# Layer-norm inputs of a second feed-forward turned by 32x32 blocks and a trip through DRAM, with three side portions per step

## The reference

```
xattn 0:  q = f(y Wq'), g = sigmoid(y Wg' + bg);  linear attention to 64 context rows; (attn * g) Wo'
ffn 0:    gelu(y proj1' + b1) proj2' + b2                       (512 -> 2048 -> 512)
xattn 1:  softmax(y ctx' / sqrt(512), masked) ctx               (64 context rows)
ffn 1:    p = softmax(y gate_w'); top 8 of 32 experts, weights summed into 8 groups: w
          out = sum over groups g of w[g] * (silu(y Gate_g') * (y Up_g')) Down_g'
          (8 groups x 192 = 1536 hidden features)
```

## Time and profile before

| | us |
|---|---|
| median of 3 runs (lowest, highest) | 1904.37 (1902.69, 1906.14) |
| the profiled execution | 1901.83 |
| its span | 1900.0 |
| TensorE busy | 1847.5 (97%) |
| VectorE busy | 995.8 (52%) |
| ScalarE busy | 539.8 (28%) |
| GpSimd busy | 323.6 (17%) |
| an F block (909.4 to 992.2 in the trace) | 82.8 |
| an E block (1291.3 to 1394.5) | 103.2 |

### The profile page before, as it was taken

One profiled execution on the slowest core, in us unless ns is written; L12 is line 12 of the kernel. 1 busy time (PEld: TensorE's weight loads), 2 busy tenths in 40 slices (PEclk: granted clock), 3 DMA queues, 4 the chain that ended last, 5 costly groups with the idle time before them and its releaser, 6 DMA issues.

```text
span 1900.0 us, 24571 instructions
## 1 busy us (share of the span) xinstructions
PE 1847.5 (97%) x9552; PEld 904.3 (48%) x9552; DVE 995.8 (52%) x2036; ACT 539.8 (28%) x801; POOL 323.6 (17%) x299
## 2 busy tenths in 40 slices
PE   6689999999999999999999999999999999999999
PEld 3355555544444444444444444444444444444444
DVE  4577776754545454554436554545545555545422
ACT  2233533411121222112112233333323333332321
POOL 1122332222020211202020011111111111111111
PEclk9899999999999999999999999999999999999999
DMA  3323443333224232332301200101010101000000
GB/s 110 91 62 106 133 148 97 100 107 77 79 61 133 60 101 89 78 105 53 89 23 40 67 9 1 54 1 53 1 53 1 53 1 54 1 23 1 1 23 22
DMA packets 135829, 112.09 MB, mean 59 GB/s; under 512 B 75554, under 2 KB 92066, under 8 KB 135714
## 3 DMA queue, kind: packets, MB, share of 16 engines
q1 hardware_dynamic: 135714, 110.53, 19.7%
HBM read 78.00 MB, written 32.51 MB: 58 GB/s over the span
## 4 chain that ended last, share of the span: by engine, by line
PE 83%; issue 9%; DVE 3%; POOL 2%; DMA 2%; ACT 1%; POOLq 0%; SPq 0%; DVEq 0%; ACTq 0%
PE bank L862 44%; PE bank L951 17%; PE bank L1031 10%; PE bank L931 4%; PE bank L871 3%; PE bank L897 2%; PE bank L916 1%; POOL arena L836 1%; PE bank L1018 1%; DVE arena L1217 1%; PE bank L966 1%; POOL arena L810 0%; PE bank L993 0%; DMA arena<-in_L_xattn_Wkv 0%; DMA arena<-x_after_ffn 0%
## 5 line engine op out<-in xcount | busy, mean ns | idle before, releaser
L862 PE MATMUL bank<-arena 128*128 128x512 f16 x4608 | 1044.5, 381 | 26.3 <-DVE arena L1284 11.2
L862 PEld LDWEIGHTS bank<-arena 128*128 128x128 f16 x4608 | 451.8, 98 | 558.8 <-issue 17.3
L951 PE MATMUL bank<-arena 128*128 128x512 f16 x1536 | 352.1, 379 | 1.3 <-DVE arena L1444 1.3
L1031 PE MATMUL bank<-arena 128*128 128x512 f16 x1152 | 264.3, 379 | 0.9 <-POOL arena L836 0.9
L1586 DVE SCALAR_TENSOR_TENSOR arena<-bank,arena 128x512 f32<-128x512 f32 x96 | 72.0, 750 | 329.0 <-PE bank L862 329.0
L1130 ACT ACTIVATE arena<-bank,arena 128x512 f32<-128x512 f32 x128 | 99.6, 778 | 489.0 <-PE bank L862 485.8
L951 PEld LDWEIGHTS bank<-arena 128*128 128x128 f16 x1536 | 150.1, 98 | 181.2 <-DVE arena L1444 1.8
L836 POOL TENSOR_TENSOR arena<-arena 128x512 f16<-128x512 f32 x96 | 111.0, 1157 | 625.9 <-ACT arena L1167 625.9
L1442 DVE TENSOR_SCALAR arena<-arena 128x512 f16<-128x512 f32 x128 | 65.7, 513 | 282.8 <-ACT arena L1130 282.5
L1031 PEld LDWEIGHTS bank<-arena 128*128 128x128 f16 x1152 | 112.0, 98 | 128.4 <-POOL arena L836 1.4
L1444 DVE SCALAR_TENSOR_TENSOR arena<-arena 128x512 f16<-128x512 f32 x128 | 118.0, 922 | 4.6
(11 more groups left out here) (159 smaller groups left out, 1213.0 us busy)
## 6 DMA issues: line engine op xcount, KB each, us to landing
arena<-in_L_ffn_proj SPq DMA_DIRECT2D x64, 256.0 KB, 2.9
arena<-in_L_ffn_gate_up_proj SPq DMA_DIRECT2D x96, 96.0 KB, 2.0
x_after_attention<-arena SPq DMA_DIRECT2D x8, 1024.0 KB, 5.2
arena<-x_after_attention SPq DMA_DIRECT2D x8, 1024.0 KB, 5.5
x_after_ffn<-arena SPq DMA_DIRECT2D x8, 1024.0 KB, 4.3
arena<-x_after_ffn SPq DMA_DIRECT2D x8, 1024.0 KB, 6.3
arena<-in_x SPq DMA_DIRECT2D x7, 1024.0 KB, 5.5
normalised_blocks<-arena SPq DMA_DIRECT2D x28, 256.0 KB, 2.0
```

What stands on the lines that cost most here:

```text
L862: m = e.matmul(bank[b][:, :], wT[l][:, c, tile * P:(tile + 1) * P], y[h][:, c, :], start=n == 0, stop=n == NPASS - 1)
L951: m = e.matmul(bank[t][:, :], hv[h][:, 0, t * P:(t + 1) * P], w2T[l][:, j, :], start=j == 0 and i == 0, stop=j == NH - 1 and i == 2)
L1031: m = e.matmul(bank[t][:, :], hv[h][:, 0, t * P:(t + 1) * P], dnT[l][:, j, :], start=j == 0 and i == 0, stop=j == NR - 1 and i == 2)
```

## The change

`in_blocks` becomes true for L and M of every batch, so their 16 normalisations take the second way. `block_tasks` is rewritten: two statistics portions, then norm, block transpose and store of one tile in one portion, the load right behind the fourth, a pause of three empty portions (two for L(0) and M(0)), `whole` in two portions and one empty one. It holds for F(1) to F(7) as well. The E loop takes a third portion, between `ge` and `ue`. The empty portions ahead of `pturn` and `rturn` change: one and two for b = 0, two and four else. The list for a batch is then 30 portions for b = 0 and 35 else.

```diff
 def in_blocks(i):
     ph, b = i
-    return ph == "F" and b > 0
+    return ph in "LM" or (ph == "F" and b > 0)
...
+    def block_tasks(i):
+        def stats(ts):
+            for t in ts:
+                add("stat", i, t)
+            if NT - 1 in ts:
+                add("rs", i)
+        def tile(t):
+            add("norm", i, t)
+            add("block", i, t)
+            add("bstore", i, t)
+            if t == NT - 1:
+                add("bload", i)
+        def whole(cs):
+            for c in cs:
+                add("whole", i, c)
+        return ([lambda: stats((0, 1)), lambda: stats((2, 3))] + [lambda t=t: tile(t) for t in range(NT)]
+                + [None] * (2 if i in (("L", 0), ("M", 0)) else 3) + [lambda: whole((0, 1)), lambda: whole((2, 3)), None])
...
-    def block_tasks(i):
-        def stats():
-            for t in range(NT):
-                add("stat", i, t)
-            add("rs", i)
-        def step(t):
-            if t < NT:
-                add("norm", i, t)
-            if t > 0:
-                add("block", i, t - 1)
-                add("bstore", i, t - 1)
-        def whole(c):
-            add("whole", i, c)
-        return ([stats] + [lambda t=t: step(t) for t in range(NT + 1)] + [lambda: add("bload", i)]
-                + [None] * 6 + [lambda c=c: whole(c) for c in range(NC)])
...
-        return [L[0], both(split, L[1]), L[2], L[3], L[4], L[5], L[6],
-                lambda: add("scores", b, banks=1), lambda: None, lambda: add("pturn", b, banks=1),
-                lambda: add("read", b, banks=NT), *M, lambda: add("router", b, banks=1), lambda: None, lambda: None,
-                lambda: add("rturn", b, banks=1)]
+        pause = [None] * (1 if b == 0 else 2)
+        return [L[0], both(split, L[1]), *L[2:], lambda: add("scores", b, banks=1), *pause,
+                lambda: add("pturn", b, banks=1), lambda: add("read", b, banks=NT), *M,
+                lambda: add("router", b, banks=1), *pause, *pause, lambda: add("rturn", b, banks=1)]
...
     while side:
-        side.pop(0)()
+        f = side.pop(0)
+        if f:
+            f()
...
             add("ge", b, j, banks=1)
+            apart()
             add("ue", b, j, banks=1)
-            if side:
-                side.pop(0)()
+            apart()
...
         if J < total and j == 0 and b + 1 < NB:
             side = attention_tasks(b + 1)
-        if side:
-            side.pop(0)()
+        apart()
```

More of the change, by code:

```diff
@@ L348, in make_plan, with apart @@
     while side:
-        side.pop(0)()
+        f = side.pop(0)
+        if f:
+            f()
     add("xload", "E", 1)
     add("xload", "E", 2)
+    def apart():
+        f = side.pop(0) if side else None
+        if f:
+            f()
     total = NB * NR
```

## The result

The changed kernel took 1922.99 us (median of 4 runs, 1918.22 to 1927.85), the kernel before 1903.53 us beside it. The ratio is 1.0099, with a 95% interval of 1.0085 to 1.0113: 19.5 us slower where 9.1 us faster was forecast, and outside the range (1884 to 1909).

The account below looks back on a forecast made before the run. TensorE, busy 97%, was taken as the bound. Turns -27.7, old wait -1.0, blocks 1 to 7 +1.5, L(0) +4.9, M(0) and router +8.9, half clock +4.3 gave -9.1 us: 1895.3 us, range 1884 to 1909.

Parts of the forecast that it names:

- What the turns are worth: L and M of all batches: 64 groups of TensorE transposes removed at 0.433 us each, 27.7 us gained.
- L(0) and the seam: Between the two feed-forwards: scores wait 4.9 us, router 2.9, its bare chain 6.0, then 4.3 us at half clock.
- The first feed-forward: F(1) to F(7): pause shrinks to three portions, but the cover holds; 0 us, at most 2.
- What may suffer is ScalarE ... 0 us, at most 2: First feed-forward: ScalarE blocked in `whole` about 13.7 us until loads land; cover to some 8 us, so 0 to 2.
- Blocks 1 to 7: Second feed-forward: L and M inputs just in time for scores and router; 1.5 us in all, bounds 0 and 21.
- The softmax and the router's chain keep 7.8 and 12.9 us before their turns; nothing.: Blocks 1 to 7: this time stands against some 6 us of work, so no cost.
- The store's 2.0 us landing: Chain through DRAM: a tile's store lands 2.07 us after its tile, freeing the buffer for a later transpose.
- 16.4 forecast: Chain from the last VectorE transpose to a usable input: 10.2 us to landed loads, 0.7 cast, 5.5 subtractions.
- the products have 2 us and more: GpSimd's 56 later subtractions could each delay a VectorE product up to 1 us; slack before the down-projection covers it.
- 0.1 us to spare: Blocks 1 to 7: scores and router inputs both met by this margin; priced at 0.1 us each, 1.5 in all.
- My own bound (21 us): Blocks 1 to 7, upper bound: 14 x 1.5 us, with subtractions at the 1.61 maximum plus 0.6 of landing.
- Rival (C): Scores and router of blocks 1 to 7 late 14 times; at 1.5 us each +10.4 us, 1914.8 us; chance 0.15.

Follow-up runs that it names:

- e5: Changed kernel with the low half of the inputs on VectorE everywhere and the router of batches 1 to 7 one portion later: 1889.23 us, ratio 0.9931.
- e1: Changed task list for F(1) to F(7) alone; L and M of all batches turned by TensorE with the old side list: 1908.63 us, ratio 1.0025.
- e4: Changed kernel with the low half of the inputs (subtraction after the cast) on VectorE instead of GpSimd everywhere: 1897.36 us, ratio 0.9965.
- e3: Changed kernel with the router of batches 1 to 7 one portion later, behind its step's down-projection: 1910.07 us, ratio 1.0044.
- e8: Changed kernel with the four statistics of L(b) and M(b), b from 1, in one portion, so tiles come one portion sooner: 1920.04 us, ratio 1.0089.
- e9: Changed kernel with the 1 MB load of x issued five steps later in the block of batches 1 to 5: 1922.46 us, ratio 1.0099.
- e10: Changed kernel with the later x load and the router one portion later, GpSimd still making the low half: 1903.78 us, ratio 1.0002.
- e7: Changed kernel with the low half of F(1) to F(7) alone on VectorE, L and M staying on GpSimd: 1922.2 us, ratio 1.0123.

## Why the prediction was wrong

**What the turns are worth: right.** 0.433 us a group. e5's block is 3.49 us shorter than before, 8 x 0.436.

**L(0) and the seam: right.** Forecast waits of 4.9, 2.9 and 6.0 us and 4.3 us at half clock; measured 4.04, 2.05 and 6.04, and 1.4 us behind the first and 2.0 behind the last in slower matmuls: 15.5 us in place of 18.1. The list's length (30 tasks for 27 portions) told it.

**The first feed-forward: wrong, 0 us forecast and 5.7 measured** (F(4); 3.87 us wait and 1.8 in slower matmuls behind it). The step "What may suffer is ScalarE ... 0 us, at most 2" asked only who waits for the loads. It left out that the shorter list moves GpSimd's subtractions to where its all-reduce follows, and the 5.8 us that GpSimd takes between the two kinds. The trace of before showed three such pauses ahead of an all-reduce, 5.9 to 6.4 us (e1), and others behind one, 7.0 us at 832 us among them.

**Blocks 1 to 7: wrong, the step that failed most: 1.5 us forecast, about 28 measured** (the 30 us that are missing in the second stage, less the 2.0 behind the seam). The scores waited 8.65 us, the router 6.3, the down-projection of step 10 8.4, and a fall of the granted clock behind a wait at 1443 us cost 1.6; the rest, some 3 us, is the part of each wait that its length doesn't count. Four claims in it failed:

- "The softmax and the router's chain keep 7.8 and 12.9 us before their turns; nothing." I asked when the chain is done, not what it stands in front of. The third portion lies between two of a step's own VectorE instructions, and e5 against e4 shows that this placing cost the waits of step 10, 8.4 us here. The router's 6.3 us, which e3 took away too, were something else: its input was late, and both a later router (e3) and an earlier input (e4, e8) free it.
- The store's 2.0 us landing was taken from a stretch without a 1 MB load beside it. The first store took 3.9 to 5.7 us in five L chains out of seven, all those with the load, and that was about half of the scores' waits (e9). From the last transpose on the chain was sized well: 15.7 to 17.1 us in the seven L chains, 16.4 forecast. But TensorE left it 13.7 to 16.0 us, as the fourth transpose came late.
- The hold of GpSimd on VectorE was seen in the rows and waved off ("the products have 2 us and more"). How much of the lateness it made stays open: e4 takes it away together with 2.2 us of the link, and in e10 it is there and five of seven blocks have no wait over 0.3 us.
- "0.1 us to spare" at 14 places was priced at 0.1 us each. Each lateness is paid in full and each earliness gives nothing, so a margin of 0.1 us with a scatter of 1 to 3 us is paid: 13 of the 14 places waited, 15.0 us in all. My own bound (21 us) was nearer than the value I took.

Rival (C) had the sign and the mechanism, "inputs late in every block", and its price per us; I gave it 0.15. The step-10 wait and the first feed-forward stood in no rival.

The parts add up: -28.7 us for what went, +15.5 for L(0) and the seam, +5.7 for the first feed-forward and +28 for blocks 1 to 7 give some +20, where the medians give +19.5. The terms for the turns and the seam were near; the two that were put at 0 and 1.5 us were not.

## What to carry to other kernels

When latency replaces work on the bound engine, count the chain link by link, and if the margin is smaller than the scatter of its DMA landings, take the wait as real at every place where it occurs. When a portion of side work gets a new place in a step, list what each engine has behind it: a 6 us chain of tiny instructions ahead of one product cost 1.2 us in each of seven blocks, though its own result wasn't wanted for another 12.9 us. The change itself was good for 23 us once its last link ran on the engine with idle time, the chain stood behind the step's own work, and the one batch whose time was too short kept the old way.

## What was not expected of the hardware

GpSimd started its all-reduce 5.83 us after a row of subtractions, with its input ready and nothing that the profile shows to wait for; after 24 us of idling the same instruction started within 0.1 us of its input (e7). The kernel before has the same pause three times in its first 175 us (5.9 to 6.4 us). A 256 KB store mostly landed in 2.0 us with no other transfer beside it, and in 3.9 to 5.7 us when it was issued 3.8 us behind a 1 MB load on the same queue.
